# A graph network on one core: matmuls into a spare PSUM bank behind every chunk of the four sum passes

## The reference, cut to what matters

```python
# block 0, twice: spline convolution: 4 weighted rows per edge, mean over the destination
msg = jnp.einsum('es,eso->eo', basis, xw[src[:, None], widx]);  agg = segment_sum(msg, dst)
# block 1: graph convolution with degree norms
out = segment_sum(norm[:, None] * x[from_], to_)
# block 2: an MLP on (source row, destination row, 32 edge features), summed per destination
messages = mlp(concat[nodes[row], nodes[col], edge_features]);  aggregated = segment_sum(messages, col)
# block 3, three times: a linear layer on (x[dst], x[src], 16 edge features), summed per destination
m = concat([x[dst_f], x[src_f], ea_f]) @ W.T + b;  agg = segment_sum(m, dst_f)
```

## Time and profile before

| | us |
|---|---|
| median of 2 runs | 20073.03 (20056.41 to 20089.66) |
| the profiled execution | 20154.05, span 20152.2 |
| PE busy | 8383.3 (42%) |
| POOL busy | 11020.9 (55%) |
| DVE busy | 4749.9 (24%) |

### The profile page before, as it was taken

How to read it: one execution, slowest core, us unless ns; L and a number is a source line. 1 busy time by engine, 2 the same in 40 slices (tenths; PEclk the granted TensorE clock), 3 DMA queues, 4 the chain that set the end, 5 groups by cost and what they waited for, 6 DMA issues and landing times.

```text
span 20152.2 us, 144869 instructions
## 1 busy us (share of the span) xinstructions
PE 8383.3 (42%) x34014; PEld 7106.5 (35%) x34014; DVE 4749.9 (24%) x7949; ACT 1130.3 (6%) x2610; POOL 11020.9 (55%) x11663
## 2 busy tenths in 40 slices
PE   7655555344443333334444443333323333333333
PEld 4333444233333333334444433333323333223333
DVE  4333333233332111112323221111121111211111
ACT  2101111000000000000111100000000000000000
POOL 0355555455555665655555556555545555465655
PEclk9877777677776555556666665555555555555555
DMA  4444444333332111113333321111111111111111
GB/s 194 151 127 143 143 145 145 99 94 95 95 95 61 26 29 29 29 36 88 88 86 87 87 64 24 23 24 23 23 25 23 23 23 23 26 24 25 26 25 24
DMA packets 1013136, 1320.35 MB, mean 66 GB/s; under 512 B 546589, under 2 KB 704574, under 8 KB 987470
## 3 DMA queue, kind: packets, MB, share of 16 engines
q0 software_dynamic: 426240, 764.57, 15.7%
q1 hardware_dynamic: 586830, 555.05, 8.6%
HBM read 970.98 MB, written 347.67 MB: 65 GB/s over the span
## 4 chain that ended last, share of the span: by engine, by line
another core or an unknown queue 57%; PE 18%; issue 13%; DVE 7%; DMA 1%; SPq 1%; DVEq 1%; ACT 1%; ACTq 0%; POOL 0%; POOLq 0%
PE PS L770 10%; PE PS L690 4%; DVE BIG L1376 2%; DVE OH L1356 1%; PE PS L699 1%; DMA AG<-acc 1%; PE PS L803 1%; PE PS L764 1%; DVE BIG L1383 1%; DVE BIG L1391 0%; DVE XC L1224 0%; PE PS L677 0%; ACT STG L971 0%; SPq L485 0%
## 5 line engine op out<-in xcount | busy, mean ns | idle before, releaser
L770 PE MATMUL PS<-BIG,OH 128*128 128x64 f32 (+3 forms) x23310 | 5742.5, 428 | 3488.2 <-DVE OH L1356 1837.9
L611 POOL DMA_INDIRECT BIG<-t_mp,IDX x4995 | 4715.1, 944 | 3512.2 <-issue 1714.7
L770 PEld LDWEIGHTS PS<-BIG,OH 128*128 128x128 f32 x23310 | 5083.9, 296 | 4025.7 <-DVE OH L1356 1884.2
L611 POOL DMA_INDIRECT BIG<-t_cell,IDX x3330 | 3151.1, 946 | 3150.7 <-issue 1795.2
L764 PE MATMUL PS<-STG,CARRY 128*128 128x64 f32 (+3 forms) x1554 | 566.5, 463 | 6424.0 <-ACT STG L971 4910.6
L1356 DVE TENSOR_TENSOR OH<-REL,PS 128x640 f32<-128x640 f32 x2331 | 1885.2, 816 | 3815.8 <-remote 3125.4
L764 PEld LDWEIGHTS PS<-STG,CARRY 128*128 128x128 f32 x1554 | 352.6, 282 | 6598.9 <-ACT STG L971 4889.6
L611 POOL DMA_INDIRECT BIG<-t_p,IDX x1665 | 1579.6, 949 | 1335.4 <-DMA IDX<-in_src 574.3
L611 POOL DMA_INDIRECT BIG<-t_gcn,IDX x1665 | 1573.9, 945 | 1092.9 <-DMA IDX<-in_src 596.6
L803 PE MATMUL PS<-BIG 128*128 128x128 f32 x3330 | 593.7, 341 | 1101.7 <-DVE BIG L1383 969.9
L1354 DVE TENSOR_SCALAR CARRY<-PS,DELTA 128x128 f32<-128x128 f32 x777 | 270.7, 348 | 3185.7 <-remote 2261.7
(11 more groups left out here) (150 smaller groups left out, 3317.2 us busy)
## 6 DMA issues: line engine op xcount, KB each, us to landing
t_cell<-BIG SPq DMA_DIRECT2D x198, 1280.0 KB, 4.5
BIG<-in_dst_row SPq DMA_DIRECT2D x333, 240.0 KB
BIG<-t_mp,IDX POOLq DMA_INDIRECT x4995
BIG<-t_cell,IDX POOLq DMA_INDIRECT x3330
BIG<-t_gcn,IDX POOLq DMA_INDIRECT x1665
BIG<-t_p,IDX POOLq DMA_INDIRECT x1665
BIG<-in_ef SPq DMA_DIRECT2D x333, 80.0 KB
BIG<-t_q SPq DMA_DIRECT2D x333, 48.0 KB
```

The source lines that it names most:

```text
L611: nc.gpsimd.indirect_dma_start(to[:, j, :], None, table, bass.IndirectOffsetOnAxis(ap=IDX[:, s // CHUNKS, at:at + 1], axis=0)).then_inc(ga ...
L770: last = nc.tensor.matmul(WIN[:, 0:out_w], OH[:, s % CHUNKS, j * P:(j + 1) * P], src[:, j, :], start=False, stop=(s % CHUNKS == CHUNKS - 1 ...
```

## The change

Behind each chunk of a sum pass, that is behind the matmul that raises `chunk_done`, PE gets four further calls. Each multiplies `IDENT` by the 192 columns of `WDS` into bank 5 and signals nobody. The other passes and all other engines are as before.

```diff
+IDLE = 4
@@ fast_pass of block.tensor, body
                     if c == 0:
                         carry(g)
                     sum_chunk(s)
+                    if kind == "sum":
+                        for j in range(IDLE):
+                            nc.tensor.matmul(bank(5, 3 * F), IDENT[:, :], WDS[:, :, :].rearrange("p l f -> p (l f)"),
+                                             start=True, stop=True)
```

## The result

| | before | after |
|---|---|---|
| median of 2 runs, us | 20073.03 | 20380.51 (20358.9 to 20402.12) |
| ratio, 95% interval | | 1.0131 (1.0107 to 1.0155) |
| span of the profiled execution, us | 20152.2 | 20357.0 |

The forecast was 20,820; the loss is 307 us between the medians (205 between the profiled executions) where I had 747. The range held the time.

A forecast was written before the change was run, and what follows sets the result against it. POOL's gathers plus index-load waits behind PE's held signals were taken to bound the kernel. Node steps +660 and other cycles +90 us on 20152.2 gave 20,902 profiled, 20,820 as median; 8-in-10 range 19,750 to 22,200.

The forecast's parts named there:

- What bounds the kernel: Sum passes: POOL's gathers, 2079 us a pass, plus 51 index-load waits, 568.6 us in pass 5, behind PE's held signals.
- Instructions since the burst began: In a burst of gathers, the count of PE instructions decides whether PE's signals are held until the burst ends.
- One instruction: A filler matmul of 192 f32 columns takes 0.33 us at the low clock, eight 2.6 us.
- PE's own time: Fillers add 866 us a pass; PE busy about 1820 us stays hidden below POOL's floor of 2079.
- The clock: PE's granted clock in the sum passes rises from 0.50 to 0.6 to 0.7.
- The node steps: Fillers push L699 behind the release in 132 node steps, 5.0 us each: +660 us.
- every group is held: Rival: each group of three chunks becomes its own cycle of 28.6 us; 21,000 to 22,300 us, chance 0.27.
- signs named beforehand: PEclk 6 or 7, index waits about 750 us a pass, L699 behind the release, passes 0, 1 and 3 unchanged.
- The mlp pass as a measure of the held case: Sum passes going at the mlp pass's 8.66 us a chunk would add 970 us.
- Faster through the clock: Rival: higher clock lets a third group finish before signals are held, bursts of nine chunks; 19,280 us, chance 0.10.
- Hidden: Rival: fillers run in PE's 28 idle us; 0 to +400 us, near 20,200, chance 0.25.

The follow-up runs named there:

- pace3: Kernel before, no fillers, with POOL writing a scratch tile three times behind each chunk's five gathers in the sum passes: 19711.27 us, 0.9809 of before.
- wide2: The change with two filler calls of 384 columns instead of four of 192, against the kernel before: 20159.42 us, 1.0027.
- narrow8: The change with eight filler calls of 96 columns instead of four of 192, against the kernel before: 21120.31 us, 1.0505.
- only23: The change with its fillers only behind slots 2 and 3 of each unit, right ahead of the node step's matmuls, against the kernel before: 19902.26 us, 1.0033.
- f2: The change with two filler calls of 192 columns behind each chunk instead of four, against the kernel before: 20105.5 us, 1.0001.
- pace3_fill4: The change plus three POOL scratch writes behind each chunk's gathers in the sum passes, against the kernel before: 19560.36 us, 0.9852.
- pace2: Kernel before with two POOL scratch writes behind each chunk's gathers in the sum passes, on two chips where nothing is held: 1.0838 and 1.0837 of before.

## Why the prediction was partly right

**What bounds the kernel** held: POOL's pace plus the waits for the index load that stand behind PE's held signals. pace3 shows it, by taking the waits away.

**Instructions since the burst began** as what matters, and not the burst's age: right in kind. The table of slow starts has one count and several ages, and wide2, the change and narrow8 show that the count matters at equal columns. Incomplete was the picture of a signal that is held while PE works on: that is the kernel before, whose bursts hold some 100 matmuls and loads in the median of pass 5 (142 after the change); past some 120 to 145 PE itself starts slowly, and the fillers queue in front. And it isn't the burst alone: on three chips bursts hold nothing. The trace of before, from one chip, could not show that.

**One instruction** at 0.33 us: measured 2890.0/10656 = 0.27 us, a mixture of both clocks. **PE's own time** hidden: right, and more so than forecast (1326 us busy in pass 5 for my 1820, since the clock rose). **The clock** at 0.6 to 0.7: right, 0.65 to 0.67, and worth nothing, as passes 1 and 3 had suggested. The Trainium skill, "TensorE: Matmul & The Clock Gate", Part 1, has sustained activity release the clock; the trace agrees, 0.50 before and 0.67 after in pass 5, and a kernel whose pace another engine sets doesn't gain by it.

**The node steps, +660 us**, are the step that failed, and it failed in its mechanism. I had each of the 132 steps lose 5.0 us, with L699 falling behind the release, where today it came through early in the burst. That was read off one cycle. In the next cycle of the same rows L699 already stood behind the release, 3 us after ACT's copies of 16146.72:

```profile
16149.49 0.63 PE L699 MATMUL PS<-WDS,HT 128*128 128x64 f32 x2
```

Counted from the trace of before, in pass 5 L699 starts more than 8 us behind L677 in 15 of the 33 steps, and DVE starts more than 8 us behind L699 in 16 others: 31 of 33 were held already. After the change not one is in pass 5; in passes 4, 5 and 6 it was 93 of 99 and is 12. DVE's idle time in front of the instruction that waits for L699 (us, times, longest), pass 5, before and then after:

```profile
DVE SQ L1326 <- remote: 597.3, 16, 38.9
DVE SQ L1326 <- PE PS L699: 388.3, 17, 26.3
```
```profile
DVE SQ L1331 <- PE PS L700: 160.7, 20, 9.5
DVE SQ L1331 <- issue: 109.0, 13, 9.4
```

986 us became 270. So the term went the other way: L699 moved ahead of the hold, and the loss came elsewhere. only23 agrees, with 50 us for the fillers in that place. (In pass 2 a step has three L677 and six L699, half of what the prediction took for all.)

What came in its place: part of the long bursts became short ones, each with a wait of its own. With pauses over 2 us, pass 5 has 34 bursts of 15 gathers after (before 3) and 37 of 30 (before 49); the short ones wait 6.9 us in the mean, the long ones 10.8. A cycle of three chunks then takes 18.7 + 6.9 = 25.6 us, 8.5 a chunk, against 8.0 for the long one. That is the rival "every group is held", in part of the cycles and at a lower price than I gave it (28.6 us a group): I took the release 5.4 us behind the last gather from long bursts, where the short one shows 3.1. In the four sum passes there are 126 short bursts where there were 16; 110 x 3 chunks at 0.5 us more are 165 us of the 221 by which these passes grew. Where the remaining 56 us come from stays open.

So of the signs named beforehand PEclk and the unchanged passes came true, L699 behind the release and 750 us of index waits did not, and that the forecast had the right direction was luck: the loss came by a mechanism to which it had given the smaller chance.

**The mlp pass as a measure of the held case** (8.66 us a chunk) was too high for the change, 2726/333 = 8.2 in pass 5; narrow8, with twice its added instructions, takes 2919/333 = 8.8.

**Rivals.** Faster through the clock: no run with a higher clock is faster for it, f2 beside wide2 and pace3 beside pace3_fill4. Hidden: true on three chips.

## What to carry to other kernels

Before adding work to an idle engine for the sake of its clock, ask which engine sets the pace; here PE's clock rose by a third and no run gained by it. Where one engine issues gathers back to back for tens of us, look in the trace at the lag between an instruction's end and the wake of its waiter, and at instructions that wait for nothing yet start in even steps: if they lag, fewer and wider instructions, or a short pause in the gathers, are worth more than a faster engine. The pause has a price where nothing lags (8% for pace2). And measure on more than one chip before tuning against such a lag.

## What the runs showed of the hardware

- On the chips of the first runs, in a stretch of POOL's indirect gathers 1.25 us apart, signals of PE came up to 30.7 us late, until 3.1 to 5.4 us after the stretch. After some 120 to 145 matmuls and loads (medians of six kernels) PE's own starts came in steps of 0.70 us: eight matmuls with their loads took 20.4 us that take 1.52 to 2.87 elsewhere. Some 1.4 us of other work on POOL behind every five gathers ended both.
- On three other chips the changed kernel shows none of it, and the kernel before takes 15850 us for 20073. What sets the two kinds of chip apart no run tells, except that the gathers' transfers take about as long on both (3155 and 3264 us). Nor is it shown what the engines contend for.
- An f32 matmul with 192 columns took 0.19 us at the high clock (eight in 1.52).
